# Softmax row sums of an attention kernel: four tiles a chunk added on GpSimd instead of summed on TensorE, and a ring of six tiles

## The reference

```python
qkv = jnp.einsum('oc,bchw->bohw', w_qkv, x)
q, k, v = map(reshape, jnp.split(qkv, 3, axis=1))       # (b, 8, 32, 4096)
scores = jnp.einsum('bhdi,bhdj->bhij', q, k) / jnp.sqrt(32.)
attn = jax.nn.softmax(scores, axis=-1)
out = jnp.einsum('bhij,bhdj->bhdi', attn, v)
x = jnp.einsum('oc,bchw->bohw', w_proj, out.reshape(b, c, h, w)) + x
```

## Time and profile before

| | us |
|---|---|
| median of 3 runs | 2951.43 (2949.24 to 2952.44) |
| profiled execution, its own time | 2950.03 |
| its span in the profile | 2948.1 |
| busy: PE / ACT / DVE / POOL | 2656.8 / 2346.0 / 2291.1 / 32.6 |
| one chunk of attention (134.39 to 202.35 us of the span) | 67.96 |
| granted clock of TensorE, mean | 0.988 |

### The profile page before, as it was taken

The page is one execution under the profiler, slowest core; times in us unless marked ns, Lnnn a source line. Parts: engine busy times, 40 slices in busy tenths (PEclk is TensorE's granted clock), DMA queues, the critical chain, the costliest instruction groups (busy, mean ns, idle before and its releaser), DMA issues. The chain is left out here.

```text
span 2948.1 us, 58305 instructions
## 1 busy us (share of the span) xinstructions
PE 2656.8 (90%) x24658; PEld 746.7 (25%) x24666; DVE 2291.1 (78%) x1446; ACT 2346.0 (80%) x2554; POOL 32.6 (1%) x140
## 2 busy tenths in 40 slices
PE   7999999988999999688979999999899999996889
PEld 4222222242212222133442222222411222222334
DVE  3888888857888888677538888888578888886765
ACT  4999999959999999428449999999499999994284
POOL 0000000000000000001000000000000000000010
PEclk9999999999999999999989999999999999999999
DMA  2000000000000000101110000000000000001011
GB/s 76 2 2 1 2 2 2 2 2 2 2 2 1 2 2 2 48 24 44 39 62 2 2 2 2 2 2 2 1 2 2 2 2 1 2 2 54 18 44 43
DMA packets 24742, 36.91 MB, mean 13 GB/s; under 512 B 10336, under 2 KB 11424, under 8 KB 24096
## 3 DMA queue, kind: packets, MB, share of 16 engines
q1 hardware_dynamic: 24480, 33.16, 3.3%
HBM read 22.88 MB, written 8.68 MB: 11 GB/s over the span
## 5 line engine op out<-in xcount | busy, mean ns | idle before, releaser
L455 ACT ACTIVATE P<-scores 128x1024 f32<-128x1024 f32 x2048 | 1988.6, 1023 | 159.3 <-PE scores L374 74.6
L485 DVE TENSOR_TENSOR acc<-acc,P 128x2048 f32<-128x2048 f32 x768 | 1711.0, 2286 | 80.3 <-ACT P L455 72.8
L385 PE MATMUL psOL<-P,V 128*32 128x512 f32 x8192 | 1091.2, 605 | 0.8 <-ACT P L455 0.8
L374 PE MATMUL scores<-Q,K 32*128 32x512 f16 x12288 | 847.7, 378 | 165.2 <-ACT P L455 49.4
L374 PEld LDWEIGHTS scores<-Q,K 32*128 32x128 f16 x12288 | 227.8, 92 | 1193.1 <-ACT P L455 1070.0
L485 DVE TENSOR_TENSOR acc<-P 128x2048 f32<-128x2048 f32 x64 | 146.7, 2292 | 243.7 <-PE psOL L403 205.1
L385 PEld LDWEIGHTS psOL<-P,V 128*32 128x32 f32 x8192 | 161.6, 108 | 438.2 <-issue 432.6
L259 PE MATMUL scores<-X,wq_sb 128*128 128x512 f32 x256 | 128.7, 633 | 42.1 <-DMA X<-in_x 29.6
L395 PE MATMUL psOL<-P,ones 128*32 128x512 f32 x1024 | 133.3, 592 | 0.0
L1014 DVE SCALAR_TENSOR_TENSOR Pl<-O,Ph 128x1536 f16<-128x1536 f32 (+1 forms) x48 | 75.9, 1581 | 65.2 <-ACT Ph L987 65.2
L980 ACT ACTIVATE O<-scores 128x1536 f32<-128x1536 f32 (+1 forms) x48 | 62.4, 1300 | 71.1 <-PE scores L915 71.1
(11 more groups left out here) (106 smaller groups left out, 1330.2 us busy)
## 6 DMA issues: line engine op xcount, KB each, us to landing
X<-in_x SPq DMA_DIRECT2D x16, 512.0 KB, 7.8
R<-att_inv SPq DMA_DIRECT2D x32, 256.0 KB
out<-res SPq DMA_DIRECT2D x32, 256.0 KB, 2.0
R<-pool_inv SPq DMA_DIRECT2D x2, 2048.0 KB, 6.9
TB<-TA SPq DMA_DIRECT2D x2, 512.0 KB, 4.4
wq_sb<-in_w_qkv SPq DMA_DIRECT2D x1, 768.0 KB, 4.6
Ls<-L SPq DMA_DIRECT2D x32, 8.0 KB
att_inv<-Ls SPq DMA_DIRECT2D x32, 8.0 KB
```

The costliest lines, as they stand in the source:

```text
L374: last = nc.tensor.matmul(dst[:, (h % 2) * CH:(h % 2 + 1) * CH], K[rows, kp, j * 128:(j + 1) * 128], Q[rows, qp, cs], start=(n == 0), stop ...
L385: last = nc.tensor.matmul(psO[h * D:(h + 1) * D, :], V[:, j, h * D:(h + 1) * D], P[:, (j % RING) * G + h, :], start=(j == 0), stop=(j == J ...
L455: nc.scalar.activation(P[:, r:r + 2, :], s3, ACT.Exp, scale=SCORE).then_inc(s_exp, 1)
L485: nc.vector.tensor_tensor(acc[:, sum_of(n)], old, new, ALU.add).then_inc(s_add, 1)
```

## The change

The four tiles that TensorE summed directly are replaced by four others, SUM_D = [5, 12, 19, 26], which GpSimd sums into a third accumulator acc[2]: the first by a copy, the other three by adds. `direct_sums` is gone. TensorE flushes three accumulators in place of two, acc[2] first, in steps 0, 1 and 2 of the next chunk. The ring P has six slots. Since 32 is no multiple of 6, a tile's slot depends on the chunk, and VectorE's loop over the chunks is written out in Python. The start values of the semaphores are gone; the first chunk leaves out the waits instead. VectorE still sums 28 tiles with 26 adds.

```diff
-RING = 4
+RING = 6
-SUM_PE = [7, 15, 23, 31]
-SUM_V = [j for j in range(JT) if j not in SUM_PE]
+SUM_D = [5, 12, 19, 26]
+SUM_V = [j for j in range(JT) if j not in SUM_D]
...
-ACC_AFTER = [JT + 1, JT + 2]
+FLUSH = [2, 0, 1]
+ACC_AFTER = [JT, JT + 1, JT + 2]
...
-                        acc = sb(c2, "acc", [128, 2, G, CH])
+                        acc = sb(c2, "acc", [128, 3, G, CH])
...
-                                def direct_sums(c, j):
-                                    if j == SUM_PE[0]:
-                                        pe.wait_ge(s_l_free, c + 1)
-                                    for h in range(G):
-                                        last = nc.tensor.matmul(psL[h * D:(h + 1) * D, :], ones[:],
-                                                                P[:, (j % RING) * G + h, :],
-                                                                start=(j == SUM_PE[0]), stop=False)
-                                    last.then_inc(s_sum, 1)
-
-                                def flush(c, k):
-                                    pe.wait_ge(s_add, (c + 2) * ADDS - 1 + k)
+                                def flush(c, i):
+                                    k = FLUSH[i]
+                                    if i == 0 and c:
+                                        pe.wait_ge(s_l_free, c)
+                                    if k == 2:
+                                        pe.wait_ge(s_psum, len(SUM_D) * (c + 1))
+                                    else:
+                                        pe.wait_ge(s_add, (c + 1) * ADDS - 1 + k)
                                     for h in range(G):
                                         last = nc.tensor.matmul(psL[h * D:(h + 1) * D, :], ones[:], acc[:, k, h, :],
-                                                                start=False, stop=(k == 1))
+                                                                start=(i == 0), stop=(i == len(FLUSH) - 1))
                                     last.then_inc(s_sum, 1)
...
+                                def slot_free(m):
+
+                                    c, j = divmod(m, JT)
+                                    act.wait_ge(s_pv, m + 1)
+                                    if j in SUM_D:
+                                        act.wait_ge(s_psum, c * len(SUM_D) + SUM_D.index(j) + 1)
+                                    else:
+                                        act.wait_ge(s_add, c * ADDS + adds_through(j))
...
+                            @block.gpsimd
+                            def _(pool):
+                                for c in range(NC):
+                                    for i, j in enumerate(SUM_D):
+                                        pool.wait_ge(s_exp, c * 2 * JT + 2 * j + 2)
+                                        r = (c * JT + j) % RING * G
+                                        if i == 0:
+
+                                            if c:
+                                                pool.wait_ge(s_sum, (c - 1) * len(FLUSH) + FLUSH.index(2) + 1)
+                                            nc.gpsimd.tensor_copy(acc[:, 2], P[:, r:r + G, :]).then_inc(s_psum, 1)
+                                        else:
+
+                                            pool.wait_ge(s_psum, c * len(SUM_D) + i)
+                                            nc.gpsimd.tensor_tensor(acc[:, 2], acc[:, 2], P[:, r:r + G, :], ALU.add
+                                                                    ).then_inc(s_psum, 1)
```

More of the change, by code:

```diff
@@ L56, in sum_of @@
 def sum_of(n):
-    return n % 2 if n < 2 else (n + ADDS) % 2
-NSUM = len(SUM_PE) + 2
-ACC_AFTER = [JT + 1, JT + 2]
+    return n % 2
+FLUSH = [2, 0, 1]
+ACC_AFTER = [JT, JT + 1, JT + 2]
 O_AT, L_AT = 3, 9
 TERMS = [(0, 0), (0, 1), (1, 0)]
-assert SUM_V[:4] == [0, 1, 2, 3] and JT % RING == 0
+assert SUM_V[:4] == [0, 1, 2, 3] and ADDS % 2 == 0
 def conv_seq(nc, x, wqkv, wproj, gw, tw, pw, ww, vectors, biases, out, r_dram, r1_dram):
@@ L441, in chunk @@
                                         j, pair = divmod(o, 2)
[L442 to L454, removed]
+                                        n = c * JT + j
+                                        act.wait_ge(s_ready, n + 1)
+                                        if pair == 0 and n >= RING:
+                                            slot_free(n - RING)
+                                        r = n % RING * G + 2 * pair
+                                        s3 = buf[(2 * n + pair) % NBUF].rearrange("p (u n) -> p u n", n=CH)
                                         nc.scalar.activation(P[:, r:r + 2, :], s3, ACT.Exp, scale=SCORE).then_inc(s_exp, 1)
@@ L463, in _, with chunk @@
                             def _(dve):
[L464 to L471, removed]
+                                def chunk(c):
                                     for n in range(ADDS):
@@ L481, in chunk @@
                                         else:
-                                            dve.wait_ge(s_add, (c + 1) * ADDS + n - (sum_of(n) != sum_of(n - 1)))
+                                            dve.wait_ge(s_add, c * ADDS + n - 1)
                                             old = acc[:, sum_of(n)]
                                         nc.vector.tensor_tensor(acc[:, sum_of(n)], old, new, ALU.add).then_inc(s_add, 1)
-                                        if n == ADDS // 2 and not first:
-                                            dve.wait_ge(s_out, 16 * (c + 1))
-                                            nc.vector.reciprocal(Ls[:, g, bass.ds(c - 1, 1), :],
-                                                                 Ls[:, g, bass.ds(c - 1, 1), :]).then_inc(s_inv, 1)
@@ L491, in _ @@
-                                chunk(0, True)
-                                with dve.Fori(1, NC) as c:
-                                    chunk(c, False)
+                                        if n == ADDS // 2 and c:
+                                            dve.wait_ge(s_out, 16 * c)
+                                            nc.vector.reciprocal(Ls[:, g, c - 1:c, :], Ls[:, g, c - 1:c, :]
+                                                                 ).then_inc(s_inv, 1)
+                                for c in range(NC):
+                                    chunk(c)
```

32 lines of the change are left out of this document (16 added, 16 removed).

## The result

The change takes 3142.71 us (median of 4 runs, 3138.55 to 3145.77) against 2951.93 for the kernel before: a ratio of 1.0645, 95% interval 1.0627 to 1.0664. The profiled execution of the change took 3145.26 us (span 3143.6), that is 195.2 more than the 2950.03 of the one before. The forecast was 3165 with turns between VectorE and GpSimd as the mechanism.

A forecast was written before the change was run, and what follows sets the result against it. ScalarE bounds the kernel now at 67.96 us a chunk; with turns VectorE would, at 58.1 + 15.9 = 74.0. That is +54 us a pass, +216 for four on 2950.0: 3166, stated as 3165, range 2865 to 3350.

The forecast's parts named there:

- the likeliest case: VectorE adds and GpSimd operations take turns, lying end to end, so VectorE sets the pace: 3165 us, chance 0.52.
- GpSimd's price: GpSimd's operations on 128x2048 f32: an add 4.5 us, a copy 2.4, together 15.9 us a chunk.
- The sum: With turns, VectorE's 58.1 plus GpSimd's 15.9 make 74.0 us a chunk, +54 a pass, +216 for four.
- The rest of the change: Direct sums, ring and loop without GpSimd disturbing VectorE: 65.3 us a chunk, 2.7 below now, 2871 us in all.
- the wait of the first flush for GpSimd: TensorE's first flush, at the new chunk's tile 0, waits for GpSimd's add of tile 26: costs nothing.
- The ring step: Six slots remove ScalarE's 2.34 us hole at tile 4 of a chunk, with 0.9 us to spare.
- The loop: Writing out VectorE's loop over chunks gains nothing; without cover by running adds, some 0.05 us an add at most.
- The clock: TensorE's slow refill at 1.2 GHz behind a pause lies under VectorE's queue of filled tiles: nothing added.
- No disturbance: Rival: VectorE and GpSimd work at once without extra cost, 65.3 us a chunk, 2871 us; chance 0.25.
- Partial turns: Rival: VectorE and GpSimd take turns only for part of a GpSimd operation, 2880 to 3050 us; chance 0.11.
- GpSimd never gets its turn: Rival: GpSimd waits while VectorE has work, until VectorE runs dry; 84.8 us a chunk, 3510 us; chance 0.12.
- VectorE's slack of 7.2 us a chunk: VectorE's idle time in a chunk of 65.3 us, beside 58.1 busy, taken as free for GpSimd's turns.

The follow-up runs named there:

- e2_memset: The change with GpSimd's copy and adds made memsets of the same tile of acc[2], same waits and writes, no reads: 2873.98 us in one run.
- e6_copies: The change with GpSimd's three adds made copies of the ring's tile to acc[2], one SBUF input: 2897.10 us in one run.
- e7_split: The change with each GpSimd operation cut into four of 128x512, one head each, same work: 3118.54 us in one run.
- e4_reduce: The change with VectorE's adds made maxima of the same new tile, one SBUF input and a 128x4 output: 2874.26 us in one run.
- e1_none: The change without GpSimd's copy, adds and the waits for them; acc[2] set once a pass and flushed as before: 2869.91 us, ratio 0.9725.
- e8_ring6_direct: The kernel before with only its ring set to six slots and VectorE's loop written out for it: 2933.91 us, ratio 0.9937.
- e9_loop_out: The kernel before with only VectorE's loop written out and the semaphores' start values gone: ratio 1.0001.
- e5_two_ops: The change with GpSimd taking only tiles 5 (copy) and 19 (add) of each chunk: 2896.59 us in one run.
- e12_pass_end: The kernel before with ring of six, no GpSimd work, direct sums only for tile 31, in each pass's last chunk 15, 27, 31: 2876.28 us, ratio 0.9743.

## Why the prediction was right

**The mechanism** was the likeliest case's: VectorE and GpSimd take turns, and VectorE sets the pace. The trace shows what was named for it: adds of 6.65 us for the forecast 6.8, GpSimd adds of 4.54 plus up to 1.8 of waiting, VectorE busy 98% of a chunk (70.40 of 72.16), ScalarE's holes of 2.7 to 2.8 in that chunk for the forecast 3. Only the forecast of four grown adds a chunk was off: three grow to 6.6, and the one beside the copy to 3.13. The Trainium skill's rule ("SBUF — State Buffer", Who interferes with whom), which no row of before could show, agrees with every run here. That GpSimd's reads count and not its writes is shown by e2_memset and e6_copies (adds of at most 2.294 and of up to 3.975 us), and that the later one waits for the whole instruction by the timelines around 197 us and by e7_split. That it takes VectorE's second SBUF input agrees with e4_reduce (at most 2.290 us), which doesn't separate it from the size of the output.

**GpSimd's price.** An add was taken at 4.5 us between bounds of 1.8 and 6.2 from rows of memsets and a select; alone it takes 4.56. A copy was taken at 2.4 and takes 1.89.

**The sum** had two errors against each other. VectorE loses 13.3 us a chunk, not 15.9. The copy has to wait for an add at the head of a chunk, and it works in part while VectorE waits 0.77 us for an exponential anyway: two adds that would take 4.5 us take 5.33 there, so it costs 0.8. A grown add takes 6.64 us in place of 2.28, so GpSimd's add costs 4.36, a little less than its own 4.56. (By durations that is 3 x 4.36 + 0.8 = 13.9. Busy time counts only once the 0.08 us by which adds without a gap overlap, and VectorE has fewer gaps now: most of the difference from 13.3.) That is 8 x 2.6 = 21 us too much a pass. On the other side VectorE idles 15 us in a pass at the starts and heads of its chunks (its waits for exponentials and flushes are 83.8 + 7.1 us, less the 7.9 ahead of each pass's first add, over four), of which I had counted 1. From its first add to the end of its last psL copy a pass grows by 47.5 us in the mean (541.3 to 588.8), not 54. The four make 190 of the 195.2 us between the two profiled executions; the other 5 lie outside the passes. The forecast was 22 us over the median. That it came so near is in part luck: the two errors, 21 us too much and 14 too little in each pass, belong to separate terms and only happen to cancel. The term that was mis-sized is "58.1 + 15.9 = 74.0"; it is 58.1 + 13.3 = 71.4 and 1 to 1.5 us of idling (72.4 in the mean of the first pass's chunks, (648.33 - 141.22) / 7, and 72.6 to 72.9 in the others).

**The rest of the change**, 65.3 us a chunk and 2871, is confirmed by e1_none, hole by hole (65.27, 2869.91), and so is the wait of the first flush for GpSimd, costed at nothing: in the change TensorE never waits for GpSimd. The ring step was right within this sum, where the flush holes were counted beside it, but "the 2.34 is the ring's" says too much: alone the ring is worth 0.7 us a chunk (e8_ring6_direct), since the two flush holes lie behind the wait.

**The loop** costs nothing (e9_loop_out). **The clock**: I added nothing for it. Behind the hole at 188.58 the granted clock was 0.53, that is 1.2 GHz, for 3 us (the second of the windows above), and VectorE stayed busy all through it, 3.20 of 3.20. At the end of a pass the flushes do take longer, as in e5_two_ops, but only by 1 to 2 us each pass.

**The rivals.** No disturbance is excluded by the adds of 6.65 us. Partial turns are excluded by e7_split and the timelines around 197 us. That GpSimd never gets its turn is excluded as well: it waited 1.8 us at most, for the add in course. What the prediction did not have is the pass end. It said VectorE's slack of 7.2 us a chunk is free, and with e5_two_ops and e6_copies it is in the middle of a pass, but not in its last chunk, where another 5 us a pass appear. In the change itself VectorE is as late: the last psL copy of the first pass waits 8.19 us, in the kernel before 1.99. The sum went by VectorE's last add and so has this wait in it; only its 1.7 us for a flush and a copy behind that add were 2.6 (655.10 to 657.70).

## What to carry to other kernels

An engine's idle time is not room for another engine's work when the instructions of the two take turns: VectorE was idle 14% of a chunk and GpSimd all of it, and 15.6 us of GpSimd work a chunk (3 x 4.56 + 1.89) cost VectorE 13.3. The same idle time served when VectorE itself took over three of the four tiles (e12_pass_end). Before moving work to GpSimd, look whether VectorE's instructions beside it have two SBUF inputs, as the adds here; if so, price the GpSimd time as VectorE time. And a wait's row names the last to come, not what the wait is worth: ask what lies behind it, and what happens at the end of the phase, where no later work covers a late engine.

## What the hardware showed that was not expected

- The turns are strict and fair, even against a VectorE queue without gaps: GpSimd never waited longer than one add (6.39 us in all for an add of 4.56), and with quarter-size pieces the two alternated, 3.31 us a piece.
- A GpSimd copy of 128x2048 f32 takes 1.89 us, hardly more than the memset of 1.81, and less than half of an add (4.56).
- TensorE's clock fell to its lower level after a pause of 2.81 us (before 189.66 us of the change's span), in a stretch in which its matmuls had come without a wait. The 12 score matmuls behind it took 1.47 us in place of 0.83. But behind a pause of 2.91 us in the same chunk (before 207.34) they took 0.83, at a granted clock of 1.00 from 207.30 to 210.30. So the length of the pause alone doesn't decide.
